# A transformer layer on eight cores: ternary weight steps placed behind the attention bias, the weights' scales worked out at the ends of two head pairs, and the first loads of the feed-forward stage spread over more slots

## The reference

```
x = x + attention(layernorm(x), W_query, W_key, W_value)   # 16 heads of 64, causal
x = x + ffn(layernorm(x), w1, conv_w, conv_b, w2)

attention: softmax(q k^T / 8, causal) v
ffn:       h = bit_linear(x, w1)               # 1024 -> 4096
           h = silu(depthwise_conv1d(h) + b)   # 3 taps along the tokens
           out = bit_linear(h, w2)             # 4096 -> 1024
bit_linear(x, w): x is rounded to 8 bits per token (scale from its largest value);
                  w becomes -1, 0 or 1 times mean(|w|) of the whole matrix
```

## Time and profile before

| | |
|---|---|
| time, median of 3 runs | 977.31 us (977.04 to 978.27) |
| the profiled execution's own time | 977.3 us |
| its longest span (core 5), the shortest | 975.7 us, 969.7 us |
| PE, DVE, ACT, POOL busy in core 5 | 91%, 73%, 71%, 64% |
| attention's first and last exponent in core 5 | 104.5 us, 466.3 us |
| feed-forward | 467.4 us to the end |

### The profile page before, as it was taken

One profiled execution on the slowest core, in us unless ns is written; L12 is line 12 of the kernel. 1 busy time (PEld: TensorE's weight loads), 2 busy tenths in 40 slices (PEclk: granted clock), 3 DMA queues, 4 the chain that ended last, 5 costly groups with the idle time before them and its releaser, 6 DMA issues.

```text
span 975.7 us, 24133 instructions; the slowest of 8 cores (969.7 to 975.7 us)
## 1 busy us (share of the span) xinstructions
PE 889.0 (91%) x7516; PEld 538.3 (55%) x7516; DVE 711.9 (73%) x1173; ACT 697.3 (71%) x1108; POOL 620.6 (64%) x819
## 2 busy tenths in 40 slices
PE   1999899999999989998776699999999999999998
PEld 0454454555554545554654466666666666666443
DVE  2677665566666676669588988989899887877651
ACT  3554698889887888988988678678777777766300
POOL 2220648574655565545546978979799797978650
PEclk9999999999998999999989899999999999999999
DMA  8952666765876777774894323325343223332121
GB/s 262 331 169 91 233 222 214 237 215 181 255 247 218 223 243 250 231 238 191 243 313 162 108 67 118 139 92 173 109 133 128 89 94 124 108 130 88 44 87 44
DMA packets 38891, 166.93 MB, mean 171 GB/s; under 512 B 4977, under 2 KB 5106, under 8 KB 30066
## 3 DMA queue, kind: packets, MB, share of 16 engines
q1 hardware_dynamic: 34354, 148.62, 47.0%
q0 software_dynamic: 4416, 16.78, 5.1%
HBM read 140.22 MB, written 25.17 MB: 170 GB/s over the span
## 4 chain that ended last, share of the span: by engine, by line
PE 75%; DVE 7%; ACT 6%; issue 6%; DMA 3%; POOL 2%; SPq 0%; DVEq 0%; ACTq 0%; POOLq 0%
PE psO L968 21%; PE psM L950 19%; PE psQK L748 11%; PE psS L806 7%; PE psPV L834 6%; PE psV L723 5%; ACT PT L1110 4%; DMA wvst<-wv 2%; DMA w1b<-t1scr 2%; PE psS L816 1%; DVE psD L1543 1%; DVE hs L1524 1%; POOL hs L667 1%; PE psK L748 1%; ACT hs L1159 1%
## 5 line engine op out<-in xcount | busy, mean ns | idle before, releaser
L1110 ACT ACTIVATE PT<-psS,nbias 128x1024 bf16<-128x1024 f32 (+1 forms) x320 | 299.9, 986 | 45.2 <-PE psS L806 27.2
L950 PE MATMUL psM<-xqT,w1b 128*128 128x258 bf16 x2048 | 242.9, 277 | 20.3 <-DVE hs L1524 16.2
L667 POOL TENSOR_TENSOR hs<-hs,tb 128x256 f32<-128x256 f32 x256 | 194.6, 784 | 68.2 <-DVE hs L1524 61.8
L950 PEld LDWEIGHTS psM<-xqT,w1b 128*128 128x128 fp8e4 x2048 | 200.7, 99 | 61.4 <-issue 24.3
L1159 ACT ACTIVATE hs<-psM,convb_s,convw_s 128x256 f32<-128x256 f32 x256 | 147.5, 576 | 86.2 <-PE psM L950 61.4
L676 POOL TENSOR_TENSOR hs<-hs,srow 128x256 f32<-128x256 f32 x240 | 178.5, 777 | 15.5 <-ACT srow L1177 15.4
L1524 DVE SCALAR_TENSOR_TENSOR hs<-psM,convw_s,hs 128x256 f32<-128x256 f32 x256 | 114.8, 476 | 23.7 <-ACT tb L1163 22.6
L1543 DVE TENSOR_REDUCE psD<-hs 128x256 f32<-128x1024 f32 x56 | 109.3, 1952 | 22.0 <-ACT hs L1170 22.0
L748 PE MATMUL psQK<-ln1T,wqkb 128*128 128x512 bf16 x480 | 124.0, 382 | 1.4 <-ACT qkO L1086 0.2
L1163 ACT ACTIVATE tb<-psM,convw_s 128x256 f32<-128x256 f32 x256 | 123.6, 483 | 0.0
L834 PEld LDWEIGHTS psPV<-vaug,PT 128*128 128x128 bf16 x2176 | 92.1, 98 | 50.8 <-issue 25.5
(11 more groups left out here) (147 smaller groups left out, 1052.8 us busy)
## 6 DMA issues: line engine op xcount, KB each, us to landing
wbuf<-w1q SPq DMA_DIRECT2D x32, 1024.0 KB, 6.3
wbuf<-w2p SPq DMA_DIRECT2D x32, 1024.0 KB, 6.7
w1b<-t1scr SPq DMA_DIRECT2D x64, 512.0 KB, 3.5
x<-x SPq DMA_DIRECT2D x16, 512.0 KB, 16.7
wqkst<-wqk POOLq DMA_DIRECT2D x16, 512.0 KB, 6.6
x1scr<-x POOLq DMA_DIRECT2D x4, 2048.0 KB, 10.0
x1g<-x1scr SPq DMA_DIRECT2D x16, 512.0 KB, 4.5
out<-x1g SPq DMA_DIRECT2D x16, 512.0 KB, 2.9
```

Of the source, the lines that this page charges most:

```text
L667: e.tensor_tensor(hs_quad(q)[:, part], hs_quad(q)[:, part], tb_quad(q)[:, part], ALU.add).then_inc(g_add, 1)
L950: inst = e.matmul(psM[j][:, 0:GRP + 2], w1b[:, at:at + 128], xqT[:, x0:x0 + GRP + 2], start=(kc == 0), stop=(kc == 7))
L1110: e.activation(out=pt_unit(u).rearrange("p (h w) -> p h w", w=512)[:, :, 128 * j:512], in_=psS[u % 2][:].rearrange("p (h w) -> p h w", w=512)[
```

## The change

There are three parts.

- The second to sixth weight steps of each of pairs 0 to 6 move from slots 9, 15, 19, 24, 29 to 11, 16, 20, 25, 30.
- The scales of the two matrices are worked out in slots 32 to 38 of pairs 2 and 4, in place of slots 8 to 17, and the waits of `norms` and `weight_sum` on them are moved by one norm computation.
- In the feed-forward stage the token tiles 7 and 8 are loaded at slots 6 and 7 (before: with tiles 5 and 6 at slot 2), the residual's first two tiles at slots 12 and 13 (before: 3), and the four parts of `w2T` at slots 4, 6, 8 and 10 (before: 5 to 8). The wait for the last stored part of x1 moves from slot 3 to slot 4.

```
-            STEPS += [UN * hp + s for s in (4, 9, 15, 19, 24, 29, 34, 39)]
+            STEPS += [UN * hp + s for s in (4, 11, 16, 20, 25, 30, 34, 39)]
...
-                        for st in range(5, 9):
-                            load_x1t(st)
-                    if G == 0 and b == 3:
+                        load_x1t(5)
+                        load_x1t(6)
+                    if G == 0 and b in (6, 7):
+                        load_x1t(b + 1)
+                    if G == 1 and b in (4, 5):
+                        load_x1g(b - 4)
+                    if 8 * G + b in (4, 6, 8, 10):
+
                         x1_spilled(e)
-                        load_x1g(0)
-                        load_x1g(1)
-                    if 5 <= 8 * G + b <= 8:
-
                         e.wait_ge(a_xqf, 2)
-                        q4 = 8 * G + b - 5
+                        q4 = 4 * G + b // 2 - 2
...
-                if d in (6, 10):
-
-                    e.wait_ge(v_fin, 3 if d == 6 else 6)
+                if d in (7, 11):
+
+                    e.wait_ge(v_fin, 3 if d == 7 else 6)
...
-                e.wait_ge(a_c, 6 if f == 0 else 10)
+                e.wait_ge(a_c, 7 if f == 0 else 11)
...
-                if (hp, s) in ((2, 11), (4, 11)):
+                if (hp, s) in ((2, 33), (4, 33)):
                     weight_sum(hp // 2 - 1)
-                if (hp, s) in ((2, 16), (4, 16)):
+                if (hp, s) in ((2, 37), (4, 37)):
                     spread_scale_w(hp // 2 - 1)
...
-                if (hp, s) in ((2, 8), (4, 8)):
+                if (hp, s) in ((2, 32), (4, 32)):
                     sum_columns(hp // 2 - 1)
-                if (hp, s) in ((2, 13), (4, 13)):
+                if (hp, s) in ((2, 35), (4, 35)):
                     mean_weight(hp // 2 - 1)
-                if (hp, s) in ((2, 17), (4, 17)):
+                if (hp, s) in ((2, 38), (4, 38)):
                     place_scale(hp // 2 - 1)
```

## The result

The changed kernel takes 973.1 us in the median; the kernel before took 978.4 beside it. The ratio is 0.9949, with a 95% interval from 0.9936 to 0.9961: about 5.0 us or 0.5% faster. I had forecast 969.8, with a range from 967.0 to 973.8. The sign and the range held; the gain is two thirds of the forecast's. One of the six runs of each kernel fell into a slower state, over 1060 us with the cores of one die at a lower clock; the ratio is that of the others.

The account below looks back on a forecast made before the run. It took ACT's stalls behind a late bias in pairs 4 and 5, and PE's wait for quad 5's block, as the loss. Core 1: 976.7 - 1.6 - 1.5 - 3.8 = 969.8 us, range 967.0 to 973.8.

Parts of the forecast that it names:

- Part 1: Attention, pairs 4 and 5: bias written ahead of the ternary step ends ACT's stall; 1.6 and 1.5 us in core 1.
- with pair 6 as the measure: Attention: pair 5 falls from 46.7 to pair 6's 45.2 us; pair 4 to 45.5, with the scales' matmuls.
- I take nothing, since it is the pair 6 case: Moved step in pairs 4 and 5: `t8s` takes 1.23 us beside POOL's additions, so no hold is counted.
- first rival: POOL holds the moved step in pairs 4 and 5, ending 2.5 us later; each pair loses about 1.0: 971.8; chance 0.17.
- What is late next: DVE behind the moved step: it ends near 294.1, before slot 13's queries (294.5) and slot 15's division; 0.4 us to spare.
- signs of being wrong: Profile after: slot 13 queries later than 14.6 us, PE waiting on quad 6 or 7's block, or a new low-clock stretch.
- Part 2: Scales moved to the ends of pairs 2 and 4: taken as zero, one root of 0.2 to 0.5 us as bound.
- The same small operations run 20 slots later, so their cost stays: Scales in pairs 2 and 4: the operations only change place, 20 slots later, at the same cost.
- Part 3: Feed-forward loads: quad 5's block lands 3.4 us earlier, PE's wait and the low clock go; 3.8 us in both cores.
- The sum: Cores 1 and 5 only: core 1 comes to 969.8 us, core 5 to 967.8; the slower, core 1, is the forecast.

Follow-up runs that it names:

- the steps alone: The kernel before with only the weight steps moved to later slots (9 to 11, 15 to 16 and so on): ratio 0.9978.
- half blocks: The changed kernel with weight blocks 32 to 63 loaded with half their columns, so not computing the reference's result: ratio 0.9911.

## Why the prediction was right, and where its sum was off

- **Part 1.** The mechanism was right: the exponent of slot 12 had waited for the bias behind the step. Its term was too large, 3.1 us for pairs 4 and 5 in core 1, where the steps alone measured 2.1 (the attention) to 2.3 (pairs 4 and 5) as a mean over the cores. The step at fault is "with pair 6 as the measure": 45.2 is not what pair 5 falls to, but 45.5, since 0.3 us at slots 8 and 10 belong to the pair; and a stall of 1.7 us gives back 0.46 in the next slot.
- **"I take nothing, since it is the pair 6 case" for the hold.** For the two operations of the step it came true, but POOL's run still held DVE for 2.6 us, now the bias, which was written 13.6 us into the pair in core 5 and not 11.3. It was the mechanism of the first rival (0.17), on another operation. Pair 6 was no measure for this: POOL adds there too, but issues no load ahead of its run. That the bias held no one up was luck; the prediction had not priced it. The Trainium skill ("SBUF — State Buffer", section "Who interferes with whom") has the order of issue decide who waits; that agrees for the bias of core 5, which came 0.13 us after the first addition, but not for the two `t1s` above that began first and were held. It gives the lock for one instruction at a time, though, while here 2.58 us cover four additions and a square. The rival's price, 1.0 us for each pair, was too high for the held bias: with the hold gone (2.6 to 0.28 us), slot 12 began no earlier.
- **What is late next.** I named the queries of slot 13 and the division, and not the loads with any price. The queries are late by 1.5 us (297.51 is 16.1 us into the pair, and I had named anything past 14.6 as a sign of being wrong), and it cost nothing visible. What cost most was the block of slot 4 in pair 4 of cores 3 and 7, some 2.7 us each, with 3.4 us at the lower clock in each, one of my signs of being wrong. These two are now the slowest in the profiled execution. The sum had no term for it: it was made for cores 1 and 5 alone. With half blocks it is gone.
- **Part 2 at zero.** Mis-sized: 0.36 us in pair 2 and 0.53 - 0.26 = 0.27 in pair 4. "The same small operations run 20 slots later, so their cost stays" fails because PE sets the pace at the end of a pair.
- **Part 3.** Right in mechanism and near in size. Quads 4 to 16 fell from 79.6 to 74.9 in core 1 and from 79.6 to 75.1 in core 5, where I had said 3.8; the mean over the cores is 2.9, since two cores had waited only 2.0 and 2.1 us for the block before and three not at all. No later block and no tile was missed.
- **The sum.** Core 1's span fell from 975.1 to 968.2, just the 6.9 us of the forecast (976.7 to 969.8), but not by its terms. The attention gave 0.8 instead of 3.1, the quads 4.7 instead of 3.8, and its attention began 1.5 us earlier. That start varies from 104.5 to 106.5 us over the cores of the kernel before and lies ahead of all that was changed, so the agreement to 0.1 us is luck. Core 5 fell by 7.6 (forecast 9.5). The slowest core decides, and it was another one: 970.6 + 1.6 is the 972.2 of the profiled execution.

## What to carry to other kernels

When an instruction is held by another engine's run, moving it puts its neighbour into the same hold; look at what stands right ahead of the run, here a DMA issue on POOL that SP can do as well. Then ask what the hold costs: the step's cost time, the bias's did not. Make the sum for every core, above all those whose loads have least in hand, since a cure for the slowest core uncovers the next. A stall's worth is its length less what the next slots give back, and small work costs nothing only where its engine isn't the one that sets the pace.

## What the runs showed of the hardware

- An operation of DVE that began at the start of POOL's run of five instructions was held to the end of the run in 111 of 115 cases when POOL had issued a DMA right ahead of it (3.74 instead of 1.23 us, 2.58 instead of 0.28), and in none of five when that issue stood earlier or there was none. In the second case the additions took 2.68 or 3.66 us instead of 1.69, and where the bias came first also the square 2.02 instead of 1.03. How the DMA issue brings this about, and why four cases escaped, isn't shown.
- Halving a block's load shortened it by a quarter, not by half: over the 256 loads of the ternary steps in all cores the median fell from 6.9 to 5.1 us in the changed kernel. The three loads of core 3 around the start of pair 4 landed in a median of 6.7 us with 512 KB and 8.0 with 1 MB. The row of the halved load, by the view that gave the one of the full load above:

```profile
DMA to landing us min/median/max: 6.2/6.7/7.9
```
